# The transposes of the convolution write PSUM in the order batch, channel, and their evictions follow that order

## What is computed

```python
c = conv1d(x, weight, groups=4, taps=9, padding=4) + ctx[:, :, None] + bias[None, :, None]
x = x + attention(c)        # 32 heads, 8 kv heads, sequence = 32 channels, hidden = 512 positions
x = x + ffn(mix(x))         # mix: a 32x32 matrix for each batch, ffn: 512x512 and LoRA experts
```

## Time and profile before

| what | value |
|---|---|
| time, median of three runs | 1854.08 us |
| the profiled execution: time, and span of its trace | 1857.97 us, 1856.2 us |
| mean granted TensorE clock, share of 2.4 GHz | 0.978 |
| first block (up to the first matmul of attention) | 0 to 121.35 us |
| TensorE busy, whole span | 1770.9 us, 95% |
| VectorE busy, whole span | 1430.6 us, 77% |
| ScalarE busy, whole span | 1281.5 us, 69% |

### The profile page before, as it was taken

One profiled execution on the slowest core, in us unless ns is written; L12 is line 12 of the kernel. 1 busy time (PEld: TensorE's weight loads), 2 busy tenths in 40 slices (PEclk: granted clock), 3 DMA queues, 4 the chain that ended last, 5 costly groups with the idle time before them and its releaser, 6 DMA issues. The chain is left out here.

```text
span 1856.2 us, 34035 instructions
## 1 busy us (share of the span) xinstructions
PE 1770.9 (95%) x14079; PEld 1026.9 (55%) x14143; DVE 1430.6 (77%) x2104; ACT 1281.5 (69%) x2090; POOL 691.9 (37%) x501
## 2 busy tenths in 40 slices
PE   8669999999999999999999999999999999679998
PEld 7635555555555555555555555555555555256665
DVE  6976777777777777777777777777777777389997
ACT  5766777777777777777777777777777777432222
POOL 0205333544353335343533354435443333233332
PEclk8989999999999999999999999999999999789999
DMA  6100010001000100010001000000000000412221
GB/s 247 35 35 12 24 35 2 13 23 35 1 13 24 36 1 13 24 35 1 13 24 35 1 13 24 35 1 15 21 1 1 1 1 1 148 35 80 80 80 46
DMA packets 24039, 58.70 MB, mean 32 GB/s; under 512 B 7256, under 2 KB 7768, under 8 KB 22608
## 3 DMA queue, kind: packets, MB, share of 16 engines
q1 hardware_dynamic: 23888, 56.55, 9.2%
HBM read 47.61 MB, written 8.93 MB: 30 GB/s over the span
## 5 line engine op out<-in xcount | busy, mean ns | idle before, releaser
L840 ACT ACTIVATE banks<-banks,ratios 128x512 f32<-128x512 f32 x768 | 476.1, 658 | 137.6 <-PE banks L612 137.3
L536 PE MATMUL banks<-hT,w_q 128*128 128x512 f16 x2048 | 529.0, 381 | 11.8 <-PEq L59 6.1
L612 PE MATMUL banks<-o_hl,w_o 128*128 128x512 f16 x2048 | 532.0, 382 | 6.4 <-DVE o_hl L731 4.5
L835 ACT ACTIVATE banks<-banks,ratios 128x512 f32<-128x512 f32 x768 | 492.9, 665 | 31.6 <-PE banks L536 20.9
L789 POOL TENSOR_TENSOR q_f<-q_f,q_sin 128x1024 f32<-128x1024 f32 x128 | 301.0, 2352 | 294.5 <-DVE q_sin L688 294.5
L688 DVE TENSOR_TENSOR q_sin<-banks,rope_q 64x1024 f32<-64x1024 f32 x256 | 312.8, 1222 | 13.4 <-POOL q_f L789 8.2
L612 PEld LDWEIGHTS banks<-o_hl,w_o 128*128 128x128 f16 x2048 | 187.5, 98 | 243.6 <-DVE accT L741 17.1
L536 PEld LDWEIGHTS banks<-hT,w_q 128*128 128x128 f16 x2048 | 191.7, 98 | 235.1 <-issue 8.0
L845 ACT ACTIVATE o_hl<-banks 128x512 f16<-128x512 f32 x256 | 139.0, 595 | 145.1 <-PE banks L596 145.1
L741 DVE SCALAR_TENSOR_TENSOR accT<-banks,scales,accT 128x512 f32<-128x512 f32 x224 | 157.9, 747 | 60.8 <-PE banks L612 55.0
L563 PEld LDWEIGHTS banks<-w_kv,hT 128*128 128x128 f16 x3072 | 183.4, 98 | 30.4 <-issue 0.6
(11 more groups left out here) (116 smaller groups left out, 1743.2 us busy)
## 6 DMA issues: line engine op xcount, KB each, us to landing
codes<-in_codes SPq DMA_DIRECT2D x40, 512.0 KB, 3.7
accT<-in_xT SPq DMA_DIRECT2D x8, 1024.0 KB, 12.0
x_f<-in_x SPq DMA_DIRECT2D x32, 256.0 KB, 2.9
out<-res SPq DMA_DIRECT2D x32, 256.0 KB, 2.1
kv_s<-in_kv_scales SPq DMA_DIRECT2D x8, 512.0 KB, 4.9
hT<-aggb_rows SPq DMA_DIRECT2D x1, 2048.0 KB, 14.4
hT<-in_base_T SPq DMA_DIRECT2D x1, 1024.0 KB, 6.4
aggw_rows<-agg_sb SPq DMA_DIRECT2D x1, 512.0 KB, 2.7
```

The costliest lines, as they stand in the source:

```text
L536: mm = pe.matmul(banks[:, tile], w_q[:, n[2], kt * RF * HD + tile * HD:kt * RF * HD + (tile + 1) * HD], hT[:, kt, hp, t0:t0 + CHUNK], star ...
L612: mm = pe.matmul(o_bank(t), w_o[:, p[2], h * D + tile * P:h * D + (tile + 1) * P], o_hl[:, op, h], start=h == 0 and op == 0, stop=op == 1, ...
L835: act.activation(banks[:, tile], banks[:, tile], ACT.Copy, scale=ratio(0, n, tile, kt)).then_inc(q_scaled[tile], 1)
L840: act.activation(o_bank(t), o_bank(t), ACT.Copy, scale=ratio(1, p, 2 * pair + t, h)).then_inc(o_scaled, 1)
```

## The change

Two places change. `turned(t)` is now a view of the bank in which the channel is the inner index, and the transpose of channel s writes every fourth word of the bank, from word s on (16 bytes apart). `in_hT` has the same order, so both evictions go through the bank in the order of its words and write four neighbouring fp16 elements (8 bytes) in `hT`, then jump 64 bytes to the next batch. `low` also reads part 0 of `hT` in that way.

```diff
@@ in_hT
         s0 = g * CG + t % 2 * 4
-        return hT[:, k, part].rearrange("p (b s) -> p s b", s=S)[:, s0:s0 + 4]
+        return hT[:, k, part].rearrange("p (b s) -> p b s", s=S)[:, :, s0:s0 + 4]
 
     def turned(t):
-        return bank[3 + t % 3].rearrange("p (s b) -> p s b", s=4)
+        return bank[3 + t % 3].rearrange("p (b s) -> p b s", s=4)
@@ turn
             for s in range(4):
-                mm = pe.transpose(bank[3 + t % 3][:, s * P:(s + 1) * P], h_f[:, u % 2, 4 * half + s], w.ident[:])
+                mm = pe.transpose(turned(t)[:, :, s], h_f[:, u % 2, 4 * half + s], w.ident[:])
```

## The result

The kernel after takes 1821.2 us (median of 4 runs, 1820.2 to 1826.5), the kernel before 1853.94 us. The ratio is 0.9828, 95% interval 0.9809 to 0.9848. So 32.7 us are saved; 36 were forecast, 1818 us in a range of 1811 to 1835.

A forecast was written before the change was run, and what follows sets the result against it. VectorE was taken as the bound in the first block, at 2.87 us a step against TensorE's 2.03. Saving 34.5 us before attention and 1.5 at its start gave 36.0, so 1854.08 became 1818 us, range 1811 to 1835.

The forecast's parts named there:

- The price of the evictions: Evictions into `hT`: 128 jumps at 3.6 or 3.8 ns plus base time, 1.14 us for `low`, 1.08 us for hi.
- step 4 to step 8 of the convolution: TensorE, first block: wait for `att_T` goes, steps 5 to 7 take 7.4 us; step 8 at 28.0 us, 8.0 saved.
- wait at the tables: TensorE before `turn(12)`: waits 4.6 us, to 46.3 us, for VectorE's 6.05 us of tables; 13.3 us saved so far.
- from that wait's end to attention: Steps 15 to 31, turns, half clock losing 2.0 us, and drain: attention starts at 86.8 us instead of 121.35.
- The transposes: TensorE's writes with a 16-byte step: 0 us more, four still taking 0.47 us; ends 0 and 65 us.
- Rivals 1 and 2: Strided transposes slow down: 0.12 us more each, 1831 us, chance 0.17; or 0.51 us more each, 1878 us, chance 0.13.
- rival 4: Evictions still pay by element, stay at 2.5 us, and VectorE remains the bound: 1854 us, chance 0.05.
- The start: TensorE's 1.45 us wait for `att_T` behind the first `low` goes; step 5 starts at 20.6 us instead of 22.05.
- The clock: TensorE's granted clock: without the idle stretch it stays at 2.4 GHz from 22 to 40 us.
- rival 3: Clock falls anyway at 22 us, half until step 8; steps 5 to 8 cost 6.5 us more: 1824 us, chance 0.12.
- Attention's start: Attention's first matmuls, at half clock before: between nothing and half of 7.4 us saved, 1.5 us taken.

The follow-up runs named there:

- run with 8 bytes: Kernel after the change, but evictions write single fp16 elements 8 bytes apart in `hT` (wrong results, timing only): 1826.4 us, ratio 0.9844 to the kernel before.
- runs of two: Kernel after the change, but a bank holds two pairs of channels and evictions write two neighbouring fp16 elements (4 bytes): ratio 0.9824 to the kernel before.
- strided projection: Kernel after the change, but attention's key projection (768 fp16 matmuls of 512 columns) writes every fourth word of its bank: 1985.5 us, ratio 1.0706 to the kernel before.
- lone fp32: Kernel after the change, but `add_ctx` goes position by position, writing single fp32 elements 512 bytes apart in `h_f`: 1821.5 us, ratio 0.9818 to the kernel before.
- lone elements 4 bytes apart: Kernel after the change, but evictions write single fp16 elements 4 bytes apart in `hT` (wrong results, timing only): 1821.8 us, ratio 0.9821 to the kernel before.

## Why the prediction was right

The mechanism is the forecast one: quick evictions free VectorE, and TensorE becomes the bound. Nearly every term of the sum stands. The price of the evictions was too high, and the gain was worked out on one execution and then taken from the median of others, as told below. The steps of the sum against the profiled execution after (1826.5 us; 1857.97 before):

| step of the sum | forecast | measured |
|---|---|---|
| `low`, hi | 1.14, 1.08 us | 0.68, 0.60 us |
| four transposes, start to start | 0.47 us | 0.48 us |
| step 4 to step 8 of the convolution | 10.4 us (17.6 to 28.0) | 10.7 us (21.04 to 31.74) |
| wait at the tables | 4.6 us | 4.53 us |
| from that wait's end to attention | 40.5 us | 40.5 us (50.17 to 90.69) |
| first matmul of attention | 86.8 us | 90.69 us |
| saved from there to the end | 1.5 us | 0.8 us |

- **What bounds the kernel.** Right: with quick evictions TensorE is the bound at 2.03 us a step. That 0.68 us came in place of 1.14 changed no step. The run with 8 bytes, 1.3 us an eviction, keeps 2.03 us a step too, but it is 5 us slower than after (two executions only). Some 2 us of this lie before attention, which starts at 89.95 us, behind a wait of 3.03 us, where four traces with quicker evictions and about the same start have 87.0 to 87.6, behind 1.7. Later the clock falls a second time, to a mean of 0.57 from 124 to 132 us, which the trace of the kernel after does not have; whether the evictions bring that about is not shown. So the steps do not change below 1.6 us an eviction, but the end of the block does a little.
- **The execution that the sum was taken from.** The sum gave 36.0 us against the profiled execution before, and 8.0 of these came up to step 8, most of them the clock's fall at 22 us. The same 36.0 was then taken from the median, 1854.08 us, though the profiled execution was 3.9 us longer. Of 43 timed executions of the kernel before, 39 have a mean granted clock of 0.980 or more, and the four below that took 1858.45 to 1860.4 us; the profiled one had 0.978. In the trace with the strided transposes alone, 1854.08 us with slow evictions, the clock stays up and attention starts at 118.31 us, not at 121.35. So the median most likely holds less of that fall, and this fits the 32.7 us measured where 36 were forecast.
- **The price of the evictions** is the term with the wrong rule. I charged a jump 3.6 ns on top of each element's time. For lone half words the runs show a price for each 16 bytes entered, paid beside the elements' own time and not on top of it; for runs of two and four it does not hold, and the general rule stays open. The size (0.46 us too high for each `low`) was covered. The Trainium skill, "Advanced Engine Details and Errata", section "SBUF Cachelines", gives lines of 16 bytes, the unit that fits here, and by it the prediction named 0.69 and 0.60, which came true. The two hits on a line that it asks for are not enough in general: half words 8 bytes apart hit each line twice and took 1294 ns.
- **The transposes.** Right that they cost nothing more, 0.48 us for four. The reason given was that a halved rate would still fit. For fp16 the rate does halve (2.76 to 5.32 us for twelve matmuls). That it halves for the fp32 transposes too, and that their weight load covers it, no run shows. The Trainium skill, "Advanced Engine Details and Errata", section "PSUM Cachelines", says that patterns that are not contiguous slow matmuls significantly: the fp16 matmuls agree, the transposes do not. Rivals 1 and 2 fall by the 0.48 us, rival 4 by the 0.68 us of `low`.
- **The start.** 3.4 of the 3.9 us missing at attention's first matmul come from before the change acts. In this execution step 3 starts at 18.90 us, before at 15.47. The data of `x` came later, and eight matmuls of line 282 took some 2.7 us in each of the first three steps (the third is the row at 15.43), as at half clock, where before the second and third step took 2.08 and 1.44 already. The granted clock does not tell this: its windows read 1.00 here. In four other traces with quick evictions (evictions alone, runs of two, strided projection, lone fp32) attention starts at 87.00 to 87.58 us, near the forecast 86.8. A fifth, lone elements 4 bytes apart, starts as late as this one (step 3 at 19.17) and has 89.38.
- **The clock.** It stayed up from 22 us to the stop at the tables, as forecast, so rival 3 falls. But the reason I gave, the wait, is not sufficient, as the run with the strided transposes shows. Without the wait the clock stayed up to the stop in all ten traces; with it, it fell in two of three, for 13 and for 3.4 us. Taking the copy out of the way alone gained 3.2 us at the median, with VectorE still the bound; by that measure some 3 of the 32.7 us come this way, and the rest is the evictions' time on VectorE.
- **Attention's start.** The clock fell there again in this execution, and 0.8 of the 1.5 us came. In the run with the evictions alone in the new order it did not fall there, so this term differs between executions.

## What to carry to other kernels

Look at the innermost step of what an engine writes to SBUF: single fp16 elements 16 bytes or more apart cost 2.5 us for 512, pairs 0.7. It was enough here to change the order in which the eviction goes through the bank, since VectorE and ScalarE read PSUM with jumps of 512 bytes for nothing; TensorE should go on writing without a step: fp16 matmuls of 512 columns took nearly twice the time with one, fp32 transposes did not. A sum taken from one profiled execution should be set against that execution, and its mean clock compared with that of the timed ones, before the gain is taken from their median. When the bound moves to another engine, cut the old one's longest piece of other work into the gaps that it now has. Here that gained 6 us more.

## What I had not expected of the hardware

- The price of narrow writes is nearly the same on VectorE and ScalarE (2461 and 2511 ns 16 bytes apart, 1294 and 1325 at 8 bytes), and it is not raised when both write at once: the first hi of the kernel before, which no `low` accompanies, took 2430 ns, and the median of all 32 is 2428.
- Width counts besides the distance: fp32 elements alone, 512 bytes apart, take 2.0 ns each, fp16 elements alone 4.8 ns.
- Nearly the same wait (1.45, 1.27 and 1.40 us) brought the clock to 1.2 GHz for some 13 us in one execution and for 3.4 us in another, and left it at 2.4 GHz in a third.
